# A written-out order of work for a two-layer image network on one Trainium2 core is replaced by another

## The chip, the cores and the metric

The kernel runs on one core of one Trainium2 chip. The metric is the device time of one execution, in microseconds (us). The core has five engines with an instruction queue each: TensorE (PE in the rows), ScalarE (ACT), VectorE (DVE), GpSimd (POOL) and SyncE (SP, which only issues DMAs here). Each engine works through its own queue in order, and semaphores hold it where it needs another engine's result.

## What is computed

The input is 32 images of 96 channels by 56 x 56 positions, fp32. Two layers follow each other. Cut to what matters:

```
x = x + conv0(ln_c(x))      # expand 96->576, SiLU, 3x3 depthwise, SiLU, squeeze-excite, project to 96, + identity
t = t + ffn0(ln_t(t))       # 96->384->96 with operands rounded to fp8 (5,2), sums to fp16
x = x + conv1(ln_c(x))      # 1x1, group norm, GELU, 4 shifted 1x1 + GELU summed, group norm, 1x1
t = t + ffn1(ln_t(t))
```

Each normalisation needs one over a square root per position (or per group). It is computed on VectorE by a seed from the bit pattern and three Newton steps.

## The kernel before, in words

Images pass through the engines as through a pipeline. An image is cut into 8 tiles of 7 rows (392 positions); the work of one image is cut into steps such as `center_a 3` or `expand 0 5`. `load_x` brings an image in; `center_a`, `var_a`, `rstd_a`, `fetch_a` and `norm_a` are the first normalisation; `expand k t` is the 1x1 expansion of 128-channel chunk k; `dw k h j` is tap j of the depthwise convolution of half an image on VectorE (lines 856 and 859), `silu2 k h` its activation on ScalarE (742); `texp` and `tconv` do the rest of the channels' convolution on TensorE; `se1` to `se3` are the squeeze-excite gate; `proj` and `x1` end the first convolution. `up`, `quant`, `down`, `add` are the two feed-forward parts (index 0 and 1). `conv1`, `stats`, `gn 0`, `gelu1`, `shift`, `combo`, `fold`, `sum`, `gn 1`, `gn_weights`, `conv3`, `x2` are the second convolution. `center`, `var`, `rstd`, `fetch`, `norm` with a first index 0, 1, 2 are the other three normalisations.

A normalisation goes round through memory. TensorE sums the squares (`var`, line 511). VectorE makes the root in 12 small operations (`rstd`: line 827, 394, 397, then three times 382, 385, 387). SyncE writes it out with four DMAs (line 409), waits for them, and reads it back tile by tile, spread over 96 partitions (line 416). VectorE then multiplies (`norm`).

The shifted copies for `combo` are made by DMA: `shift t` is five issues on SyncE (lines 471, 475 and 479 for two of the three channel groups) into one of two buffers. `combo t` (line 663) is 12 matmuls into three PSUM banks; ScalarE takes each out with a GELU (line 810), `fold t` (673) adds them up in one of three ring banks, and ScalarE copies that out (814). `combo t+1` may write a bank only when the GELU of tile t has read it, and `shift t+2` may start only when `combo t` is done.

On GpSimd there are two kinds of steps: `norm_a`, which adds a tile of x and a normalised tile (line 1001, called the sums here) once VectorE's `norm_a` of the tile is done, and the clearing of the borders of `g`, three memsets (995 to 997). `save_s` on SyncE (496) writes each sum out.

What sets the order is a table of numbers, `TIMES`. For each engine it gives each step a planned time; one period of 10,000 units is one image. `timetable` sorts the steps of all 32 images by that number, `LEAD` tells which image a step belongs to in a period, and `with_banks` deals out the three ring banks of PSUM by the planned times of their readers. Nothing but the sequence that comes out of the sort is used: no engine waits for a planned time, only for semaphores. A ScalarE function of another table set makes the compiler put an `ACT_TABLE_LOAD` ahead of it; SiLU and GELU stand in different sets.

```
                plan[engine] += [(PERIOD * m + time, m - lead_of(family), step) for m in range(NIMG)]
        plan[engine].sort()
...
            bank = min(free, key=lambda b: free[b])
```

Of the kernel before, what the change touches and what calls it, by code (L numbers as in the profile page):

```python
# [48 lines left out]
        "save_s": (6456, 7078, 7232, 7410, 7684, 7737, 7794, 8398), "texp 0": (11803, 11912, 12045, 12071),
        "texp 1": (12393, 12616, 12761, 12864), "texp 2": (13722, 13815, 13896, 13976),  # L50
        "fetch_s": (17257, 17333, 19025, 19039, 19566, 19591, 20287, 20676), "rstd 0": (21298,),
        "fetch 0": (21449, 21469, 21745, 21801, 22028, 22091, 22241, 22366), "rstd 1": (22875,),
# [1149 lines left out]
```

How the kernel before makes its waits and increments, by code:

```python
    def wait_sums(pe, prev):  # L334
        if prev is None:
            return
        (name, *a), i = prev
        if name == "var_a":
            pe.wait_ge(sem["seed_a"], at(3 * (i + 1) + 1))
        elif a[0] == 0:
            pe.wait_ge(sem["seed_c"], at(3 * i + 1))
        else:
            pe.wait_ge(sem["seed_b"], at(3 * (2 * (i - 1) + a[0] - 1) + 1))
# [1 line left out]
    def wait_bank(pe, prev):  # L346
        if prev is None:
            return
        (name, *a), i = prev
        if name == "center_a":
            pe.wait_ge(sem["squared_a"], at(NT * (i + 1) + a[0] + 1))
        elif name == "center":
            L, t = a
            pe.wait_ge(sem["squared_b" if L else "squared_c"], at(NT * (2 * (i - 1) + L - 1 if L else i) + t + 1))
        elif name == "expand":
            k, t = a
            pe.wait_ge(sem["activated1"], at(N_EXP * (i + (k < AHEAD)) + NT * k + t + 1))
        elif name == "texp":
            pe.wait_ge(sem["t_activated"], at(N_TE * i + SLOTS * a[0] + a[1] + 1))
        elif name == "tconv":
            pe.wait_ge(sem["t_activated2"], at(N_TC * i + PH * a[0] + a[1] + 1))
        elif name == "down":
            pe.wait_ge(sem["down_evacuated"], at(NT * (2 * (i - 1 - a[0]) + a[0]) + a[1] + 1))
        elif name == "fold":
            pe.wait_ge(sem["z_stored"], at(NT * (i - 1) + a[0] + 1))
        elif name == "se1":
            pe.wait_ge(sem["se_scalar"], at(2 * i + 1))
        elif name == "se2":
```

## Time and profile before

| | |
|---|---|
| median of 3 runs | 7031.78 us (7015.9 to 7036.94) |
| the profiled execution's own time | 7010.7 us |
| its span | 7008.9 us |
| TensorE busy (matmul) | 5784.1 us, 83% |
| VectorE busy | 5549.2 us, 79% |
| ScalarE busy | 4280.4 us, 61% |
| GpSimd busy | 337.2 us, 5% |
| mean granted TensorE clock | 0.943 of full speed |

Busy time counts instructions on the engine. "Idle before" is time in which an engine had nothing running, with what ended it. SPq rows are issues of DMAs on SyncE; an issue occupies the queue for the time shown, and the data land later.

### The profile page before, as it was taken

The page shows a single profiled execution, that of the slowest core. Times are in us where ns is not written, and L with a number is a line of the kernel's source. Part 1 is how long each engine was busy: PE and PEld are TensorE (multiplying, and loading weights), DVE is VectorE, ACT ScalarE, POOL GpSimd, SP SyncE. Part 2 cuts the span into 40 slices and gives each one's busy share as a digit, 9 for nine tenths or more (in the row PEclk, how much of TensorE's full clock was granted, in tenths as well). Part 3 has the DMA queues.
Part 4 walks back from the last instruction along what each step waited for, and adds up shares of the span by engine and source line. Part 5 has one row for each costly group of instructions (what it writes and reads, how often), then busy time and mean ns, then how long its engine had stood idle before and what let it go on. Part 6 is the DMA issues. An engine that isn't in the chain of part 4 may idle for free. (4 is left out here: it accounts for less than half of the span.)

```text
span 7008.9 us, 111308 instructions
## 1 busy us (share of the span) xinstructions
PE 5784.1 (83%) x40192; PEld 2345.7 (33%) x40192; DVE 5549.2 (79%) x9325; ACT 4280.4 (61%) x7549; POOL 337.2 (5%) x366
## 2 busy tenths in 40 slices
PE   2788888888898888888888888888888888888875
PEld 0233333333333333333333333333333333333332
DVE  5778887788887778887888888788888878887763
ACT  1456766666766656766666766656766656766654
POOL 1000000000000000000000000000000000000000
PEclk9899999999999999999999999999999999999997
DMA  1223323333323333323333323233323333323322
GB/s 40 60 73 86 87 75 85 79 78 88 89 73 87 78 80 87 88 74 86 79 80 87 89 74 88 76 80 87 89 75 86 81 76 87 89 72 87 79 59 63
DMA packets 395480, 556.44 MB, mean 79 GB/s; under 512 B 71490, under 2 KB 391427, under 8 KB 391771
## 3 DMA queue, kind: packets, MB, share of 16 engines
q1 hardware_dynamic: 394940, 549.32, 31.0%
q8 instruction: 330, 5.41, 0.3%
q14 instruction: 210, 1.72, 0.1%
HBM read 233.66 MB, written 78.68 MB: 45 GB/s over the span
## 5 line engine op out<-in xcount | busy, mean ns | idle before, releaser
L859 DVE SCALAR_TENSOR_TENSOR conv<-mid,w_dw,conv 128x1568 f32<-128x1568 f32 x1536 | 2837.6, 1847 | 28.1
L663 PE MATMUL b_banks<-shifted,w_combo 128*32 128x392 f32 x6144 | 637.4, 539 | 280.6 <-DMA shifted<-g 233.5
L535 PE MATMUL bank<-xc_a,w_exp 128*128 128x392 f32 x1536 | 706.3, 570 | 187.1 <-DVE xc_a L842 120.3
L583 PE MATMUL bank<-conv,w_proj_gated 128*96 128x392 f32 x2048 | 729.8, 499 | 5.9 <-DVE w_proj_gated L871 5.9
L598 PE MATMUL bank<-x,centering 128*96 128x392 f32 x1536 | 655.8, 519 | 92.0 <-ACT phases L722 52.7
L775 ACT ACTIVATE hidden<-b_banks 128x1176 f16<-128x1176 f32 x512 | 590.5, 1153 | 179.0 <-PE b_banks L618 175.8
L782 ACT ACTIVATE hidden<-hidden 128x1176 fp8e5<-128x1176 f16 x512 | 604.5, 1188 | 44.9 <-PE bank L627 24.5
L715 ACT ACTIVATE mid<-bank 128x392 f32<-128x392 f32 x768 | 381.1, 497 | 373.8 <-PE bank L535 350.5
L691 ACT ACTIVATE g<-bank 96x392 f32<-96x392 f32 x512 | 254.0, 496 | 520.9 <-PE bank L598 467.8
L742 ACT ACTIVATE conv<-conv,bn_affine 128x1568 f32<-128x1568 f32 x192 | 324.9, 1692 | 329.1 <-DVE conv L859 328.7
L914 DVE TENSOR_SCALAR hidden<-hidden,b_q 128x392 f16<-128x392 f16 x1536 | 395.0, 313 | 131.1 <-ACT hidden L775 130.8
L535 PEld LDWEIGHTS bank<-xc_a,w_exp 128*128 128x128 f32 x1536 | 286.9, 210 | 508.3 <-issue 292.1
L557 PE MATMUL bank<-phases_on,w_toeplitz 128*32 128x392 f32 x4608 | 443.6, 531 | 4.0 <-DMA phases_on<-phases 4.0
L663 PEld LDWEIGHTS b_banks<-shifted,w_combo 128*32 128x32 f32 x6144 | 212.4, 116 | 650.7 <-DMA shifted<-g 410.2
L1001 POOL TENSOR_TENSOR x<-x,xc_a 96x392 f32<-96x392 f32 x256 | 317.7, 1246 | 2291.6 <-DVE xc_a L842 2291.6
L583 PEld LDWEIGHTS bank<-conv,w_proj_gated 128*96 128x96 f32 x2048 | 321.3, 163 | 298.2 <-issue 257.2
L557 PE MATMUL bank<-phases,w_toeplitz 128*32 128x392 f32 x4608 | 411.6, 494 | 1.6 <-ACT phases L722 1.0
L627 PE MATMUL bank<-hidden,w_q 128*96 128x392 fp8e5 x1536 | 353.4, 340 | 63.6 <-ACT hidden L782 45.9
L618 PE MATMUL b_banks<-xn,w_q 128*128 128x392 fp8e5 x1536 | 346.0, 334 | 65.6 <-ACT hidden L775 37.8
L842 DVE TENSOR_TENSOR xc_a<-xc_a,r_a 96x392 f32<-96x392 f32 x256 | 167.6, 665 | 261.0 <-DMA r_a<-rstd_row_a 260.7
L733 ACT ACTIVATE conv<-bank,bn_affine 128x392 f32<-128x392 f32 x384 | 261.0, 680 | 178.8 <-PE bank L557 178.4
L544 PE MATMUL bank<-xc_a,w_exp 128*32 128x448 f32 x3072 | 348.5, 548 | 22.1 <-ACT phases L722 16.7
(157 smaller groups left out, 7926.6 us busy)
## 6 DMA issues: line engine op xcount, KB each, us to landing
phases_on<-phases SPq DMA_DIRECT2D x768, 101.5 KB, 2.6
...
shifted<-g SPq DMA_DIRECT2D x256, 199.5 KB, 2.9
...
r_a<-rstd_row_a SPq DMA_DIRECT2D x256, 147.0 KB, 2.9
x_plus_norm<-x SPq DMA_DIRECT2D x256, 147.0 KB, 2.6
r_a<-x_plus_norm SPq DMA_DIRECT2D x256, 147.0 KB, 2.3
```

Source lines behind the costliest of these rows:

```text
L535: mm(ring[bank][:, 0:TW], WEXP[:, 128 * k:128 * k + 128], xc_tile(t, 128), start=True, stop=True)\
L544: last = mm(ring[bank][32 * q:32 * q + 32, 0:EROWS * WW], WEXP[:, m0:m0 + 32], xc_phase(q, h), start=True, stop=True)
L557: last = mm(ring[bank][32 * p:32 * p + 32, 0:TW], TWZ[:, (3 * g + dx) * 2 + r % 2, :], phase_rows(EB if r < 2 else FB, p, QH, dx), start=( ...
L583: mm(o, WPS[:, k, :], tile(conv(k, t // NTH, parity), t % NTH, 128), start=(k == 0), stop=False)
L598: mm(ring[bank][0:C, 0:TW], CEN[:, :], tile(XFULL[1 - parity if L else parity], t, 128), start=True, stop=True)\
L627: last = mm(ring[bank][0:C, 0:TW], W2Q[:, f, c, :], Q8[t % 2][:, c, :], start=(c == 0), stop=(c == NHC - 1))
L663: last = mm(rows(PB[32 * u:32 * u + 32, m, 0:TW]), WC[:, u // 2, 32 * m:32 * m + 32], SH[t % 2][:, u, :].rearrange("p (h w) -> p h w", w=G ...
L715: f(mid_rows((k + (k < AHEAD) + parity) % 2, 1 + ROWS * t, ROWS), rows(ring[bank][:, 0:TW]), ACT.Silu)\
L775: f(Y16[t % 2][:, :, :], PB[:, 0:NHC, 0:TW], ACT.Copy).then_inc(sem["up_evacuated"], 1)
L782: f(Q8[t % 2][:, :, :], Y16[t % 2][:, :, :], ACT.Copy, saturate=False)\
L859: v.scalar_tensor_tensor(out=acc, in0=src, scalar=WDW[:, k, j:j + 1], in1=acc, op0=ALU.mult, op1=ALU.add).then_inc(sem["convolved"], 1)
L914: last = v.tensor_scalar(Y16[t % 2][:, c, :], Y16[t % 2][:, c, :], B1Q[:, g, c:c + 1], 0.0, ALU.add, ALU.max)
```

## The change

Only the table `TIMES` is replaced, on all five engines (lines 48 to 122). No instruction of the program is written otherwise: `ITERS` is 3 on both sides, so every root still has its nine Newton operations behind the first three. The number of instructions of a kind is the same on TensorE, VectorE, GpSimd and SyncE. The sequence on GpSimd is the same too. Two of the rows, and the shortest table whole:

```
     "SP": {
-        "load_x": (2489,), "rstd_a": (6044,), "fetch_a": (6093, 6329, 6392, 6436, 6587, 6728, 6856, 7150),
+        "load_x": (1832,), "rstd_a": (4902,), "fetch_a": (4931, 5374, 5857, 5900, 6400, 6627, 6900, 6929),
...
-        "shift": (24280, 24537, 24766, 24807, 24939, 25277, 25313, 25954), "rstd 2": (28475,),
+        "shift": (24665, 24876, 24982, 25058, 25721, 25722, 26264, 26463), "rstd 2": (28520,),
...
     "POOL": {
-        "norm_a": (4007, 4903, 5096, 5325, 5773, 6384, 8893, 9938), "gn 0": (23979,)},
+        "norm_a": (12718, 12775, 12862, 12887, 12912, 13053, 16342, 17167), "gn 0": (27816,)},
```

**SyncE, around the write of `rstd_row_a`** (the root of `rstd_a`; `shifted` are the copies for `combo`, `r_a` the root read back, `x_plus_norm` the stored sums). Before:

```order
L471 DMA shifted<-g 32x4x399
L475 DMA shifted<-g 32x399
L479 DMA shifted<-g 32x3x399
L475 DMA shifted<-g 32x399
L479 DMA shifted<-g 32x3x399
L409 DMA rstd_row_a<-rstd_a 8x98 x4
L416 DMA r_a<-rstd_row_a 96x392 x4
L496 DMA x_plus_norm<-x 96x392
L416 DMA r_a<-rstd_row_a 96x392 x3
```

and with the new table, from the last issue of `shift 1` on:

```order
L479 DMA shifted<-g 32x3x399
L409 DMA rstd_row_a<-rstd_a 8x98 x4
L416 DMA r_a<-rstd_row_a 96x392
L471 DMA shifted<-g 32x4x399
L475 DMA shifted<-g 32x399
L479 DMA shifted<-g 32x3x399
L475 DMA shifted<-g 32x399
L479 DMA shifted<-g 32x3x399
```

Before, all eight shifts stand ahead of the write of the root; now two do, and six stand behind it, with reads of `r_a` among them.

**VectorE, from the root of `rstd_a` to the first products with it** (`conv` are taps of the depthwise convolution, `xc_a` the product of `norm_a`, `bn_stats` the step `sum`). Before:

```order
L387 SCALAR_TENSOR_TENSOR rstd_a<-newton_a,rstd_a 128x98
L859 SCALAR_TENSOR_TENSOR conv<-mid,w_dw,conv 128x1568 x4
L979 BN_STATS bn_stats<-g 96x6
L859 SCALAR_TENSOR_TENSOR conv<-mid,w_dw,conv 128x1568
L842 TENSOR_TENSOR xc_a<-xc_a,r_a 96x392
L859 SCALAR_TENSOR_TENSOR conv<-mid,w_dw,conv 128x1568
L979 BN_STATS bn_stats<-g 96x6
L842 TENSOR_TENSOR xc_a<-xc_a,r_a 96x392
L979 BN_STATS bn_stats<-g 96x6
L842 TENSOR_TENSOR xc_a<-xc_a,r_a 96x392
```

and now:

```order
L387 SCALAR_TENSOR_TENSOR rstd_a<-newton_a,rstd_a 128x98
L859 SCALAR_TENSOR_TENSOR conv<-mid,w_dw,conv 128x1568 x3
L842 TENSOR_TENSOR xc_a<-xc_a,r_a 96x392
L859 SCALAR_TENSOR_TENSOR conv<-mid,w_dw,conv 128x1568
L856 TENSOR_SCALAR conv<-mid,w_dw 128x1568
L859 SCALAR_TENSOR_TENSOR conv<-mid,w_dw,conv 128x1568 x4
L842 TENSOR_TENSOR xc_a<-xc_a,r_a 96x392
L859 SCALAR_TENSOR_TENSOR conv<-mid,w_dw,conv 128x1568 x2
L842 TENSOR_TENSOR xc_a<-xc_a,r_a 96x392
```

The root itself now stands 3 taps behind `gn 0`, not 12, and taps, not `sum`, stand between the products.

**ScalarE, the second half of the combos** (`gelus` and `hidden` are written by the GELUs of `combo` 4, 6 and 5, 7; `g` by `fold`, `mid` by `expand`, `conv` by `silu2`). Before:

```order
L810 ACTIVATE hidden<-b_banks 128x392 x3
L742 ACT_TABLE_LOAD
L742 ACTIVATE conv,pool_sums<-conv,bn_affine 128x1568
L814 ACTIVATE g<-bank 96x392
L810 ACT_TABLE_LOAD
L810 ACTIVATE gelus<-b_banks 128x392 x3
L814 ACTIVATE g<-bank 96x392
L810 ACTIVATE hidden<-b_banks 128x392 x3
L715 ACT_TABLE_LOAD
L715 ACTIVATE mid<-bank 128x7x56
```

and now:

```order
L742 ACTIVATE conv,pool_sums<-conv,bn_affine 128x1568
L810 ACT_TABLE_LOAD
L810 ACTIVATE gelus<-b_banks 128x392 x3
L814 ACTIVATE g<-bank 96x392
L715 ACT_TABLE_LOAD
L715 ACTIVATE mid<-bank 128x7x56
L747 ACTIVATE x<-bank,x 24x1
L810 ACT_TABLE_LOAD
L810 ACTIVATE hidden<-b_banks 128x392 x3
L715 ACT_TABLE_LOAD
L715 ACTIVATE mid<-bank 128x7x56
```

Before, one image has 6 table loads; now it has 10, all ten between `gn 0` and `gn 1` (189 in the whole program before, 311 now). On TensorE, five more steps of `expand 0`, `se2` and a `texp` now stand ahead of `gn 1`, and `proj 0` right behind it.

## Rows read from the trace of the kernel before

**Rows 1.** The page: busy time of each engine, share of the span, instructions
```profile
PE 5784.1 (83%) x40192; PEld 2345.7 (33%) x40192; DVE 5549.2 (79%) x9325; ACT 4280.4 (61%) x7549; POOL 337.2 (5%) x366
```
**Rows 2.** VectorE's first step of the gate (`se2`, line 863), once per image
```profile
L863 DVE TENSOR_TENSOR gate<-bank,b_se x32: 148/150/156, 257.3 to 6775.3; 128x5 f32<-128x5 f32 x32
```
**Rows 3.** Windows: start:end and length, PE, PEld, DVE, ACT, POOL busy, PEclk, DMA share, GB/s
```profile
3000.00:3210.00 210.00, 180.06 (x1256) 73.39 (x1254) 170.89 (x290) 133.26 (x235) 10.14 (x11) 0.94 0.32 82
3137.00:3193.00 56.00, 39.38 (x374) 15.26 (x373) 44.63 (x62) 37.82 (x65) 6.59 (x5) 0.84 0.49 110
```
**Rows 4.** Waits: engine and line <- who was waited for: total us, times, longest
```profile
DVE xc_a L842 <- DMA r_a<-rstd_row_a: 260.7, 73, 10.2
PE b_banks L663 <- DMA shifted<-g: 233.5, 151, 9.2
PE sums_b L646 <- DVE gn_small L946: 171.7, 64, 6.6
PE bank L535 <- DVE xc_a L842: 120.3, 60, 20.0
```
**Rows 5.** Timeline of VectorE: start, us, instruction, [idle before <- releaser]
```profile
3141.08 0.15 DVE L966 TENSOR_TENSOR gn_small<-v_l,gn_small 96x1 f32<-96x1 f32 x1
...
3165.07 0.26 DVE L387 SCALAR_TENSOR_TENSOR rstd_a<-newton_a,rstd_a 128x98 f32<-128x98 f32 x1
...
3182.37 0.56 DVE L842 TENSOR_TENSOR xc_a<-xc_a,r_a 96x392 f32<-96x392 f32 x1 [7.39 <-DMA r_a<-rstd_row_a]
...
3185.09 0.89 DVE L842 TENSOR_TENSOR xc_a<-xc_a,r_a 96x392 f32<-96x392 f32 x1
...
3192.31 0.37 DVE L946 BATCH_NORM_AGGREGATE gn_small<-bn_stats 96x2 f32<-96x48 f32 x1
```
**Rows 6.** Timeline of SyncE's queue, issues of DMAs
```profile
3144.16 0.64 SPq L471 DMA_DIRECT2D shifted<-g  x1
...
3176.12 1.56 SPq L409 DMA_DIRECT2D rstd_row_a<-rstd_a  x4
3178.80 0.78 SPq L416 DMA_DIRECT2D r_a<-rstd_row_a  x2
```
**Rows 7.** Timeline of TensorE, 3182 to 3202
```profile
3182.99 0.93 PE L535 MATMUL bank<-xc_a,w_exp 128*128 128x392 f32 x2 [1.42 <-DVE xc_a L842]
3186.04 1.67 PE L535 MATMUL bank<-xc_a,w_exp 128*128 128x392 f32 x2 [2.13 <-DVE xc_a L842]
...
3192.73 0.48 PE L646 MATMUL sums_b<-gn_small,mean_w 96*96 96x1 f32 x2 [2.77 <-DVE gn_small L946]
...
3201.87 1.27 PE L573 MATMUL bank<-x 24*128 24x1 f32 x10
```
**Rows 8.** Timeline of ScalarE around a table load
```profile
3150.18 0.19 ACT L733 ACTIVATION_READ_ACCUMULATOR conv<-bank,bn_affine 128x1 f32 x1
3150.40 1.28 ACT L810 ACT_TABLE_LOAD   x1
3151.69 1.28 ACT L810 ACTIVATE gelus<-b_banks 128x392 f32<-128x392 f32 x3
```
**Rows 9.** Groups of instructions: busy us, mean ns | idle before <- releasers
```profile
L715 ACT ACTIVATE mid<-bank 128x392 f32<-128x392 f32 x768 | 381.1, 497 | 373.8 <-PE bank L535 350.5 <-DVE conv L859 17.8
L742 ACT ACTIVATE conv<-conv,bn_affine 128x1568 f32<-128x1568 f32 x192 | 324.9, 1692 | 329.1 <-DVE conv L859 328.7
L804 ACT ACTIVATE g<-g,gn_small 96x784 f32<-96x784 f32 x128 | 126.0, 1032 | 6.4 <-DVE gn_small L966 6.0
```
**Rows 10.** Timeline of GpSimd, the first two sums of an image
```profile
3183.01 2.55 POOL L1001 TENSOR_TENSOR x<-x,xc_a 96x392 f32<-96x392 f32 x1 [52.48 <-DVE xc_a L842]
3186.07 1.01 POOL L1001 TENSOR_TENSOR x<-x,xc_a 96x392 f32<-96x392 f32 x1 [0.50 <-DVE xc_a L842]
```
**Rows 11.** Lines 859 and 842 on VectorE: duration ns minimum/median/maximum
```profile
L859 DVE SCALAR_TENSOR_TENSOR conv<-mid,w_dw,conv x1536: 1825/1850/2481, 134.0 to 6748.8; 128x1568 f32<-128x1568 f32 x192
L842 DVE TENSOR_TENSOR xc_a<-xc_a,r_a x256: 539/561/1370, 124.3 to 6572.6; 96x392 f32<-96x392 f32 x128
```

More of the change, by code:

```diff
@@ L47 @@
     "SP": {
-        "load_x": (2489,), "rstd_a": (6044,), "fetch_a": (6093, 6329, 6392, 6436, 6587, 6728, 6856, 7150),
[L49 to L52, printed above, removed]
@@ L53 @@
-        "fetch 1": (23421, 23468, 23500, 23694, 23795, 23804, 23816, 24004),
-        "shift": (24280, 24537, 24766, 24807, 24939, 25277, 25313, 25954), "rstd 2": (28475,),
-        "fetch 2": (29254, 29708, 30046, 30181, 30549, 30641, 30643, 30686),
-        "store": (31436, 31483, 31621, 31905, 32012, 32030, 32068, 32260)},
-    "PE": {
-        "center_a": (4070, 4733, 4772, 5057, 5214, 5262, 5266, 5383),
-        "var_a": (4752, 5199, 5201, 5275, 5309, 5403, 5603, 5866),
[6 rows of a table removed]
-        "proj": (18219, 18289, 18966, 19097, 19214, 19315, 19579, 20019),
[7 rows of a table removed]
-        "combo": (25552, 25585, 25836, 26019, 26230, 26289, 26408, 26488),
[6 rows of a table removed]
@@ L81 @@
-    "ACT": {
-        "center_a": (4379, 4389, 4571, 4828, 4851, 5099, 5146, 5402),
[13 rows of a table removed]
-        "combo": (25304, 25315, 25637, 25816, 26032, 26199, 26239, 26348),
-        "fold": (25540, 26080, 26131, 26183, 26218, 26295, 26694, 26722),
[4 rows of a table removed]
-    "DVE": {
-        "rstd_a": (6141,), "norm_a": (6569, 6723, 6864, 7166, 7202, 7462, 7998, 8010),
[17 rows of a table removed]
+        "load_x": (1832,), "rstd_a": (4902,), "fetch_a": (4931, 5374, 5857, 5900, 6400, 6627, 6900, 6929),
+        "save_s": (5677, 6677, 6723, 6855, 7082, 7091, 7815, 8098), "texp 0": (8799, 9304, 10303, 10366),
@@ new lines @@
+        "texp 1": (11310, 11671, 11721, 12321), "texp 2": (13348, 13418, 13488, 13551),
+        "fetch_s": (17458, 17933, 18453, 18458, 18703, 18742, 19029, 19049), "rstd 0": (20616,),
+        "fetch 0": (20784, 20831, 20837, 20843, 21157, 21301, 21302, 21694), "rstd 1": (22328,),
+        "fetch 1": (23260, 23290, 23343, 23381, 23422, 23460, 23664, 24595),
+        "shift": (24665, 24876, 24982, 25058, 25721, 25722, 26264, 26463), "rstd 2": (28520,),
+        "fetch 2": (28558, 28645, 28683, 28721, 29544, 30077, 30293, 30355),
@@ new lines @@
+        "store": (30260, 30746, 30809, 30936, 31085, 31161, 31687, 31821)},
+    "PE": {
+        "center_a": (2930, 3375, 3666, 3845, 3961, 3995, 3996, 4332),
+        "var_a": (3849, 3859, 3904, 4073, 4097, 4335, 4336, 4364),
[14 rows of a table added]
+        "combo": (24379, 24390, 24475, 24764, 25147, 25452, 25664, 26125),
[6 rows of a table added]
+    "ACT": {
+        "center_a": (3485, 3805, 3930, 4351, 4378, 4548, 4596, 4650),
[13 rows of a table added]
+        "combo": (25176, 25335, 25376, 25414, 25883, 26039, 26540, 26805),
+        "fold": (25278, 25839, 25946, 26117, 26395, 26634, 27208, 27210),
[4 rows of a table added]
@@ L121 @@
+    "DVE": {
+        "rstd_a": (4562,), "norm_a": (4688, 5183, 5364, 5669, 5951, 6083, 6315, 6746),
[17 rows of a table added]
     "POOL": {
-        "norm_a": (4007, 4903, 5096, 5325, 5773, 6384, 8893, 9938), "gn 0": (23979,)},
+        "norm_a": (12718, 12775, 12862, 12887, 12912, 13053, 16342, 17167), "gn 0": (27816,)},
 }
```

107 rows, old and new, of the table TIMES are left out of this document.

## Prediction

> **What bounds the kernel now.** I read the busy times first, then windows of one image, then the waits, then the timeline of the stretch where the waits are. No engine is full: TensorE is busy 83%, VectorE 79%, ScalarE 61% [rows 1]. The gate's first step runs once per image, from 257.3 to 6775.3 us, so an image takes (6775.3 - 257.3) / 31 = 210.3 us [rows 2]; filling and emptying the pipeline are the other 491 us. In 210 us TensorE works 180 and VectorE 171 [rows 3]. So the time is set by TensorE's 180 us plus the 30 in which it stands still, and a new order can only take from those 30; VectorE's 39 idle us cost something only where TensorE waits for it.
>
> TensorE's idle time is not spread evenly. In the 56 us around the stretch from `gn 0` to `gn 1` it works 39.4, and so stands still 16.6 us [rows 3], over half of all. The waits say why: for shifted copies 233.5 us in the run (7.3 an image), for the statistics of the two group norms 171.7 (5.4), for the first products `xc_a` 120.3 (3.8) [rows 4]. Behind the last stands SyncE. VectorE has the root of `rstd_a` at 3165.3 [rows 5], but SyncE is issuing shifts from 3144.16 on, forty DMAs of 0.64 us and less, and comes to the root only at 3176.12; the first product starts at 3182.37, after 7.39 us of waiting [rows 5, 6]. That is the place the new order rearranges most.
>
> **The change part by part.** Let T be the end of `gn 0` on VectorE, 3141.2. Before, `gn 1` begins at 3192.3 [rows 5], T + 51.1. I follow the new order through this stretch with the durations of the rows.
>
> 1. SyncE. Shifts 0 and 1 go out as before, till about T + 9.7. The root now stands 3 taps behind `gn 0`: 5.6 us, then 3.4 for its 12 operations, T + 9.4. SyncE writes it at once, waits as before (3176.12 to 3178.80, 2.7 us [rows 6]) and reads tile 0 at T + 12.4. The first product can run at T + 16, where it ran at T + 41.2 [rows 5]. The price: shift 2 starts at T + 12.8 where it started at T + 10.5, so the six later shifts are 2.3 us late, and the reads of `r_a` among them (0.3 to 0.4 each) add about 1.5.
>
> 2. VectorE. The 7.39 us wait goes, since 3 taps (5.6 us) now cover most of the way through memory. That is not on the path by itself; it lets `expand 0` start earlier. The two waits of `expand 0` for products, 1.42 + 2.13 [rows 7], go with it, and five more of these steps (0.92 us each, from 0.93 in [rows 7]), `se2` (1.27 [rows 7]) and one `texp` (0.9) fill TensorE's gaps before `gn 1`. Two pieces leave the stretch, a `tconv` (2.2) and a `var_a` (0.4). Net, 4.6 + 1.3 + 0.9 - 2.6 = 4.2 us of TensorE's work per image moves from where it is full to where it waits.
>
> 3. ScalarE. Here the change costs. Ten table loads stand in the stretch, not six; a load takes 1.28 us [rows 8], so 5.1 us more, and a further `silu2` comes in (1.69 + 0.19 [rows 8, 9]) for a `tconv` that leaves (0.9). ScalarE's work there: 24 GELUs, 8 copies of `fold`, 6 of `expand` and 6 operations of `center_a` at 0.50 at most 11.9 + 3.9 + 3.0 + 2.9, three `silu2` 5.6, four `gelu1` 4.1 [rows 9], small ones 0.5, loads 12.8; in all 44.7 us, where the same count gives 36.4 before (the window has 37.8 [rows 3]). Followed through, `combo 1` waits for ScalarE's extra `silu2` and load till T + 13.5; `combo 4` starts at T + 25.4; `silu2 2 1` and a load hold `se1` and `combo 7` till T + 39.8; the last `fold` is out at T + 51.3, and `gn 1` begins at T + 52.3: 1.2 us later than before.
>
> After a load the next function starts at once: the load ends at 3151.68 and the GELU begins at 3151.69, so a switch costs 1.3 us [rows 8]. The Trainium skill (ScalarE: Activation LUTs, What ACT_TABLE_LOAD costs) states 1.28 us for the load and a drain of about 1.38 behind it, 2.66 for each switch. The load agrees with this trace; the drain does not show in it.
>
> 4. The group norms. Before, `gn 1` cost TensorE 2.77 us at its first step [rows 7]; now `texp 0 0` and `expand 0 6` stand ahead and `proj 0` behind. For `gn 0` a tap no longer stands between the last `stats` and the sum. Of the 5.4 us an image [rows 4] I take 1.5 outside the stretch's length.
>
> 5. The sums on GpSimd. Beside a tap a sum took 2.55 us, beside short steps 1.01 [rows 10]; a product next to a sum took 0.89 where 0.56 is the median, a tap at most 2.48 where 1.85 is [rows 5, 11]. Eight sums now meet mostly taps: from 0 to 8 x 0.63 = 5.0 us an image on VectorE, against 0.8 before (mean 665 less 561 ns, times 8). I take no difference: VectorE waits in this stretch anyway, and nobody waits long for the sums. The Trainium skill (SBUF — State Buffer, SBUF: two separate sides) says that a VectorE operation with two SBUF inputs and a GpSimd operation that reads SBUF exclude each other for the whole instruction. A tap has two such inputs, so by that rule moving the sums from products to taps frees nothing, which speaks against this part; the 2.55 us agree.
>
> 6. The roots. No operation of a root is added or removed, so this is worth nothing. Were two Newton operations of each really gone, it would be 4 x 2 x 0.3 + 2 x 2 x 0.19 = 3.2 us of VectorE an image.
>
> 7. The rest of the image (159 us before). I compared the order there without finding a place that is clearly better or worse: the taps of the first half now lie among the products of `norm 2`, where VectorE waited, but outside the stretch TensorE works 180.1 - 39.4 = 140.7 of 154 us [rows 3], and a wait of VectorE's mostly costs nothing. I take 0, with 3 us to each side.
>
> The sum for an image: +1.2 (stretch longer) - 4.2 (work no longer to be done outside it) - 1.5 = -4.5 us. Times 31 that is -140; filling and emptying I leave as they are. From the profiled execution's 7010.7 us this gives 6871. The median of the runs, 7031.8, lies 21 above that execution, so I put the forecast between, at 6880: 1.9% below 7010.7.
>
> **The rivals.**
>
> A. Slower: ScalarE sets the stretch. It would have 44.7 us of work in 52, and the loop combo - GELU - next combo and the three ring banks leave it little room to work ahead. If the loads and the extra `silu2` all lie on the loop, the stretch grows by 5.1 + 1.9 = 7.0 us, and the fillers gain nothing, since ScalarE must empty their banks too: +7.0 - 1.5 = +5.5 an image, 7181; if the fillers still count, 7.0 - 4.2 - 1.5 = +1.3, 7051. It decides once ScalarE idles under about 4 us in the stretch. For it: the loads are certain. Against: before, ScalarE idled 18 of the 56 us. I take 7110 for this case.
>
> B. No change: SyncE is only reshuffled. What the early root gains (3.6 us of waiting for products) is lost again by the late shifts (2.3 + 1.5 = 3.8). Then 7010, give or take 20.
>
> C. Faster than forecast: the rest of the image also loses waits, half of TensorE's 13 us there (154 - 140.7). That is -4.5 - 6.5 = -11 an image, 6670.
>
> D. A switch costs more than the load itself, as where something must drain first. With 1.4 us more for each of four added loads, +5.5 on the path, the sum becomes +1.0 an image, 7042. The rows show 0.01 us behind the load, so this has 1 in 100. It is what the drain of the Trainium skill's page would do.
>
> **How the numbers follow.** About 0.3%, 21 us, is what a measurement can tell from no change. Forecast 0.50 (6780 to 6970), A 0.23, B 0.11, C 0.15, D 0.01. Faster: 0.50 + 0.15 + 0.02 of B = 0.67. Same: 0.09 of B + 0.01 of A = 0.10. Slower: 0.22 of A + 0.01 = 0.23. The range is 6690 to 7110: it leaves out the slower half of A (0.11) and the faster half of C (0.07). The forecast's own range is 6780 to 6970.
>
> **What would show it.** Right: an image takes about 206 us; VectorE's 7.39 us wait for `r_a` is near 1; the root is written within 2 us of its end; TensorE works 42 to 43 us in the stretch from `gn 0` to `gn 1`, which is 51 to 54 long; ScalarE has 311 table loads of 1.28 us, and idles some 7 us of the stretch. Wrong: a stretch of 57 us or more with waits of TensorE for GELUs (A), waits for shifted copies grown by as much as those for products fell (B), or a gain outside the stretch (C).

## The result, and the profile after

| | before | after |
|---|---|---|
| median of 4 runs on one chip | 7034.36 us | 6854.82 us (6850.41 to 6863.16) |
| ratio, 95% interval | | 0.9749 (0.9734 to 0.9764) |
| the profiled execution's span | 7008.9 us | 6852.4 us |
| mean granted TensorE clock | 0.943 | 0.959 |

The new order is 2.5% faster. The prediction said faster, 1.9%, at 6880 us. The two profiled executions are 2.2% apart, since that of before, at 7010.7 us, is faster than any of the four runs of its kernel (7015.9 to 7041.9). Up to the experiments the text compares these two. The page after, first part, which answers to [rows 1]:

```profile
PE 5730.9 (84%) x40192; PEld 2277.5 (33%) x40192; DVE 5543.4 (81%) x9325; ACT 4409.0 (64%) x7671; POOL 452.6 (7%) x366
```

ScalarE has 122 instructions more (the table loads) and 129 us more of busy time, GpSimd 115 us more for the same 366 instructions, and TensorE 53 us less for the same 40192 matmuls. Each of the three is taken up below.

Where in the run did the time go? The end of `gn 0` on VectorE (T of the prediction) comes once per image. Cut at the first and at the 31st of these, the run falls into filling, 30 whole images, and emptying (start:end and length; PE, PEld, DVE, ACT, POOL busy; PEclk, DMA share, GB/s). First before:

```profile
0.00:396.10 396.10, 211.54 (x1396) 81.09 (x1400) 259.38 (x326) 124.97 (x248) 32.58 (x33) 0.90 0.19 50
396.10:6718.20 6322.10, 5384.14 (x37666) 2189.90 (x37662) 5153.71 (x8671) 4010.42 (x7072) 304.30 (x330) 0.95 0.32 82
6718.20:7008.90 290.70, 188.39 (x1142) 74.71 (x1134) 136.09 (x330) 144.98 (x230) 0.30 (x3) 0.81 0.26 64
```

and after:

```profile
0.00:391.80 391.80, 209.49 (x1433) 81.30 (x1433) 260.37 (x328) 126.38 (x249) 33.15 (x33) 0.91 0.20 50
391.80:6563.40 6171.60, 5336.27 (x37630) 2124.45 (x37626) 5149.26 (x8671) 4135.18 (x7191) 419.16 (x330) 0.97 0.33 84
6563.40:6852.40 289.00, 185.11 (x1134) 71.79 (x1134) 133.72 (x328) 147.41 (x232) 0.30 (x3) 0.82 0.27 64
```

The 30 images are 150.5 us shorter: 5.0 an image, from 210.7 to 205.7. The filling is 4.3 shorter and the emptying 1.7. In the middle TensorE's work falls by 1.6 us an image and its idle time from 6322.1 - 5384.1 = 938.0 us to 835.3, 3.4 an image. So nearly a third of the gain, as TensorE's time is booked, is no waiting: the same matmuls take less time. (The gate's rows of [rows 2] are no fair mark for a comparison of the two orders. The last of them stood 57.1 us behind the last `gn 0` used here and stands 41.4 behind it now, so a cut there gives 5.4 us an image, and an emptying that seems 14 us longer.)

The next cut is by stage, two windows of one image on each side: from the end of `gn 0` to `gn 1`, and from there to the next `gn 0`. Before:

```profile
3141.20:3192.30 51.10, 35.66 (x350) 13.39 (x342) 41.46 (x44) 34.62 (x59) 6.55 (x5) 0.87 0.52 118
3192.30:3353.10 160.80, 145.08 (x910) 60.39 (x914) 130.27 (x247) 99.20 (x178) 3.59 (x7) 0.97 0.26 70
```

After:

```profile
2862.70:2913.10 50.40, 37.24 (x338) 13.83 (x334) 42.25 (x47) 41.00 (x66) 12.65 (x7) 0.90 0.58 141
2913.10:3067.60 154.50, 139.68 (x924) 56.61 (x922) 129.49 (x244) 96.68 (x175) 1.31 (x4) 1.00 0.25 66
```

The same two cuts over all 30 images, as the sums that close the two answers. The stretches, before and after:

```profile
sum 1520.40, PE 1038.52 PEld 384.27 DVE 1244.94 ACT 1034.11 POOL 196.61; mean PE 34.62 PEld 12.81 DVE 41.50 ACT 34.47 POOL 6.55
sum 1530.90, PE 1147.28 PEld 426.76 DVE 1265.75 ACT 1236.39 POOL 379.91; mean PE 38.24 PEld 14.23 DVE 42.19 ACT 41.21 POOL 12.66
```

and the rest of each image, before and after:

```profile
sum 4801.70, PE 4345.62 PEld 1805.63 DVE 3908.76 ACT 2976.31 POOL 107.69; mean PE 144.85 PEld 60.19 DVE 130.29 ACT 99.21 POOL 3.59
sum 4640.70, PE 4188.99 PEld 1697.69 DVE 3883.51 ACT 2898.79 POOL 39.25; mean PE 139.63 PEld 56.59 DVE 129.45 ACT 96.63 POOL 1.31
```

The stretch takes 50.7 us before and 51.0 after: it is not shorter. TensorE worked 34.6 of it and now 38.2, so it stands idle 12.8 us there where it stood 16.1, 3.3 less. The rest of the image went from 160.1 to 154.7, and this is the whole gain: TensorE has 5.2 us less work there (3.6 of it stands in the stretch now), and its idle time there is what it was (15.2 and 15.1). The granted clock of the rest rose from 0.97 to 0.99 of full speed. Less idle time in the stretch (3.3), less outside it (0.1) and less work in all (1.6) are the 5.0 us.

Where most of the work became cheaper is one line. TensorE's `expand` (line 535), as a group (busy us, mean ns | idle before <- releasers), before:

```profile
L535 PE MATMUL bank<-xc_a,w_exp 128*128 128x392 f32 x1536 | 706.3, 570 | 187.1 <-DVE xc_a L842 120.3 <-ACT mid L715 57.3 <-ACT phases L722 6.7
```

and after:

```profile
L535 PE MATMUL bank<-xc_a,w_exp 128*128 128x392 f32 x1536 | 654.9, 525 | 110.1 <-DVE xc_a L842 34.0 <-ACT mid L715 25.7 <-ACT sq_b L692 19.9
```

51.4 us less for the same 1536 matmuls, the largest fall of any line. That it nearly equals TensorE's 53.2 in the whole run is chance, since other lines changed both ways: the matmuls of a `combo` (line 663) went from 539 to 580 ns on average, half of those of line 557 (`tconv`) from 531 to 494. In the timeline of before, three steps of `expand 0` stand right behind `gn 1`, where TensorE has just waited and the granted clock is 0.50, the lower of its two levels (1.2 GHz); after, three such steps stand ahead of `gn 1` and run at the upper (2.4 GHz) at nearly twice the speed. Over 30 images of before, the `expand` matmuls in the first 6 us behind the start of `gn 1` took 862 ns on average; after, none stands there, and those in the stretch take 551. The rows of the three steps, before and after:

```profile
3194.30 4.27 PE L535 MATMUL bank<-xc_a,w_exp 128*128 128x392 f32 x6
```

```profile
2908.08 2.30 PE L535 MATMUL bank<-xc_a,w_exp 128*128 128x392 f32 x6 [0.35 <-DVE gate L863]
```

**The hand-made timeline of the stretch**, against the trace of after. With T = 2862.7, the end of `gn 0`, SyncE, then VectorE, ScalarE and TensorE read:

```profile
2864.38 0.65 SPq L471 DMA_DIRECT2D shifted<-g  x1
...
2871.74 1.44 SPq L409 DMA_DIRECT2D rstd_row_a<-rstd_a  x4
...
2874.31 0.31 SPq L416 DMA_DIRECT2D r_a<-rstd_row_a  x1
...
2875.01 0.59 SPq L471 DMA_DIRECT2D shifted<-g  x1
```

```profile
2871.29 0.26 DVE L387 SCALAR_TENSOR_TENSOR rstd_a<-newton_a,rstd_a 128x98 f32<-128x98 f32 x1
...
2877.11 0.56 DVE L842 TENSOR_TENSOR xc_a<-xc_a,r_a 96x392 f32<-96x392 f32 x1
...
2907.77 0.16 DVE L863 TENSOR_TENSOR gate<-bank,b_se 128x5 f32<-128x5 f32 x1 [1.80 <-PE bank L573]
...
2913.08 0.37 DVE L946 BATCH_NORM_AGGREGATE gn_small<-bn_stats 96x2 f32<-96x48 f32 x1
```

```profile
2872.51 1.28 ACT L810 ACT_TABLE_LOAD   x1
2873.80 0.89 ACT L810 ACTIVATE gelus<-b_banks 128x392 f32<-128x392 f32 x2
...
2898.10 1.70 ACT L742 ACTIVATE conv<-conv,bn_affine 128x1568 f32<-128x1568 f32 x1 [1.07 <-DVE conv L859]
...
2904.69 0.25 ACT L747 ACTIVATE x<-bank,x 24x1 f32<-24x1 f32 x1
```

```profile
2887.99 2.18 PE L663 MATMUL b_banks<-shifted,w_combo 128*32 128x392 f32 x24 [0.62 <-DMA shifted<-g]
...
2901.85 3.19 PE L663 MATMUL b_banks<-shifted,w_combo 128*32 128x392 f32 x24 [0.84 <-ACT gelus L810]
```

| milestone | by hand | measured |
|---|---|---|
| root written by SyncE | T + 9.4 to 9.7 | T + 9.0 |
| read of tile 0 | T + 12.4 | T + 11.6 |
| shift 2 | T + 12.8 | T + 12.3 |
| first product | T + 16 | T + 14.4, with no wait |
| combo 4 | T + 25.4 | T + 25.3 |
| combo 7 | T + 39.8 | T + 39.2 |
| `gn 1` | T + 52.3 | T + 50.4 |

The root is written 0.2 us after its end (2871.29 + 0.26), where it had waited 10.8 us behind forty issues [rows 5, 6]. The first product no longer waits. Of the waits of [rows 4], after:

```profile
DVE xc_a L842 <- DMA r_a<-rstd_row_a: 122.6, 97, 5.3
PE b_banks L663 <- DMA shifted<-g: 257.8, 151, 9.3
PE b_banks L618 <- ACT hidden L775: 116.8, 133, 2.3
```

VectorE waits 138 us less for `r_a`, while TensorE waits 24 us more for shifted copies, the price of the interleaving. The 171.7 us for `gn_small` of line 946 [rows 4] have shrunk to 8.5; a wait of `up` (line 618) for ScalarE's `hidden`, 37.8 us before, has grown to 116.8.

### The profile page after: what moved, and what is told of

Read it like the earlier page. It is cut to its first block, busy times and chain, and to the rows that moved or that the text cites. A ratio compares the mean times of both kernels' runs of the same rounds, so it can differ in the third digit from the quotient of the medians.

```text
span 6852.4 us, 111430 instructions
## 1 busy us (share of the span) xinstructions
PE 5730.9 (84%) x40192; PEld 2277.5 (33%) x40192; DVE 5543.4 (81%) x9325; ACT 4409.0 (64%) x7671; POOL 452.6 (7%) x366
## 4 chain that ended last, share of the span: by engine, by line
PE 45%; DVE 31%; ACT 10%; DMA 6%; issue 5%; SPq 4%; DVEq 0%; ACTq 0%; POOL 0%; POOLq 0%
DVE conv L859 16%; PE bank L583 10%; PE bank L598 6%; PE bank L557 4%; PE bank L535 3%; PE bank L585 3%; PE b_banks L682 3%; PE b_banks L639 2%; PE bank L544 2%; DVE hidden L914 2%; PE b_banks L663 2%; ACT hidden L782 2%; PE b_banks L618 2%; DVE xn L906 2%; DVE x L924 2%
## 5 line engine op out<-in xcount | busy, mean ns | idle before, releaser
L859 DVE SCALAR_TENSOR_TENSOR conv<-mid,w_dw,conv 128x1568 f32<-128x1568 f32 x1536 | 2893.7, 1884 | 20.4
L663 PE MATMUL b_banks<-shifted,w_combo 128*32 128x392 f32 x6144 | 681.1, 580 | 311.9 <-DMA shifted<-g 257.8
L535 PE MATMUL bank<-xc_a,w_exp 128*128 128x392 f32 x1536 | 654.9, 525 | 110.1 <-DVE xc_a L842 34.0
L782 ACT ACTIVATE hidden<-hidden 128x1176 fp8e5<-128x1176 f16 x512 | 607.4, 1186 | 39.4 <-DVE hidden L914 39.2
L1001 POOL TENSOR_TENSOR x<-x,xc_a 96x392 f32<-96x392 f32 x256 | 433.2, 1693 | 1729.9 <-DVE xc_a L842 1729.9
L722 ACT ACTIVATE phases<-bank 128x448 f32<-128x448 f32 x384 | 208.5, 543 | 515.5 <-PE bank L544 422.6
L618 PE MATMUL b_banks<-xn,w_q 128*128 128x392 fp8e5 x1536 | 348.4, 336 | 133.8 <-ACT hidden L775 116.8
L544 PE MATMUL bank<-xc_a,w_exp 128*32 128x448 f32 x3072 | 381.7, 555 | 58.2 <-ACT phases L722 47.6
L557 PE MATMUL bank<-phases_on,w_toeplitz 128*32 128x392 f32 x4608 | 411.5, 494 | 0.2 <-ACT conv L733 0.2
L691 ACT ACTIVATE xc<-bank 96x392 f32<-96x392 f32 x256 | 125.5, 490 | 434.5 <-PE bank L598 301.9
L535 PEld LDWEIGHTS bank<-xc_a,w_exp 128*128 128x128 f32 x1536 | 259.0, 193 | 377.6 <-issue 245.1
```

Source lines behind the costliest of these rows:

```text
L535: mm(ring[bank][:, 0:TW], WEXP[:, 128 * k:128 * k + 128], xc_tile(t, 128), start=True, stop=True)\
L544: last = mm(ring[bank][32 * q:32 * q + 32, 0:EROWS * WW], WEXP[:, m0:m0 + 32], xc_phase(q, h), start=True, stop=True)
L557: last = mm(ring[bank][32 * p:32 * p + 32, 0:TW], TWZ[:, (3 * g + dx) * 2 + r % 2, :], phase_rows(EB if r < 2 else FB, p, QH, dx), start=( ...
L618: last = mm(PB[:, c, 0:TW], W1Q[:, f, 128 * c:128 * c + 128], XN8[t % 2][:, :], start=True, stop=True)
L663: last = mm(rows(PB[32 * u:32 * u + 32, m, 0:TW]), WC[:, u // 2, 32 * m:32 * m + 32], SH[t % 2][:, u, :].rearrange("p (h w) -> p h w", w=G ...
L782: f(Q8[t % 2][:, :, :], Y16[t % 2][:, :, :], ACT.Copy, saturate=False)\
```

## The experiments

Twelve kernels. Each changes single numbers of the table, or one line, of the kernel after or before, so that a step stands elsewhere in one or two queues. The columns are the median, the ratio to before on the same chip with its interval, the period (from the first to the 31st end of `gn 0`, over 30), and in it TensorE's work and idle time per image, from the same window. The runs come from several chips, on which the kernel before had medians of 7017 to 7034 us. So kernels are compared by the ratio; the last three columns, each from one execution, can differ by some 0.5 us for that alone.

| run | us | ratio | period | work | idle |
|---|---|---|---|---|---|
| before | 7034 | 1 | 210.7 | 179.5 | 31.3 |
| after | 6855 | 0.9749 (0.9734 to 0.9764) | 205.7 | 177.9 | 27.8 |
| e2_root_early (of before) | 6983 | 0.9936 (0.9913 to 0.9959) | 209.7 | 180.1 | 29.5 |
| e3_gn0_first (of before) | 7103 | 1.0109 (1.0087 to 1.0131) | 213.9 | 178.8 | 35.1 |
| e1_root_late | 7140 | 1.0163 (1.0142 to 1.0184) | 215.0 | 180.1 | 34.9 |
| k_read_behind_shift2 | 6955 | 0.9898 (0.9882 to 0.9915) | 208.9 | 178.6 | 30.3 |
| i_fillers_behind_gn1 | 7010 | 0.9987 (0.9977 to 0.9998) | 210.8 | 180.4 | 30.4 |
| j_tconv_inside | 6848 | 0.9759 (0.9736 to 0.9782) | 205.5 | 176.5 | 29.0 |
| f4_four_loads | 7036 | 1.0020 (1.0008 to 1.0032) | 211.6 | 180.6 | 30.9 |
| f3_combo7_late_se1 | 6949 | 0.9908 (0.9891 to 0.9926) | 208.8 | 180.3 | 28.6 |
| f12_six_loads | 6931 | 0.9882 (0.9861 to 0.9902) | 208.0 | 178.4 | 29.5 |
| f2_late_silu2 | 6867 | 0.9781 (0.9758 to 0.9804) | 206.0 | 177.9 | 28.0 |
| g_small_sums | 6834 | 0.9747 (0.9724 to 0.9770) | 205.0 | 177.3 | 27.6 |
| h_two_newton | 6830 | 0.9726 (0.9704 to 0.9749) | 204.8 | 177.7 | 27.2 |

### One part of the change alone: SyncE's root (e2)

In the kernel before, the write of the root and its first read are moved ahead of the last two shifts.

```diff
-        "load_x": (2489,), "rstd_a": (6044,), "fetch_a": (6093, 6329, ...
+        "load_x": (2489,), "rstd_a": (5300,), "fetch_a": (5301, 6329, ...
```

> The order before, with one thing moved on SyncE alone: the write of the root of rstd_a and the read of its first tile stand ahead of shifts 6 and 7, not behind them. My theory (term 1 and 2 of the sum): VectorE's wait of 7.4 us for r_a and TensorE's two waits for products (1.4 + 2.1 us) go, and shifts 6 and 7 come 3 us later; I expect 0 to -2 us an image, 6950 to 7010 us against a before of about 7010. Rival B (SyncE is only reshuffled: late shifts cost what the early root gains): 7010 within 20 us.

The first product comes at T + 34.3 instead of T + 41.2, and its waits drop from 260.7 to 160.1 us; the rows of the first two products:

```profile
2949.69 0.56 DVE L842 TENSOR_TENSOR xc_a<-xc_a,r_a 96x392 f32<-96x392 f32 x1
2956.00 0.56 DVE L842 TENSOR_TENSOR xc_a<-xc_a,r_a 96x392 f32<-96x392 f32 x1 [3.51 <-DMA r_a<-rstd_row_a]
```

The period falls by 1.1 us, as expected, and the stretch from 50.7 to 49.5 on average. So this part of the move of SyncE's root is neither a mere reshuffling (rival B) nor, alone in the old order, the bulk of the gain: a fifth of it by the period, a quarter by the ratio.

### One part alone: `gn 0` ahead of the last tap (e3)

```diff
-        ... "gn 0": (25175,),
+        ... "gn 0": (25010,),
```

> The order before, with gn 0 on VectorE moved ahead of the last tap of dw 1 1, as the new table has it: one tap, 1.85 us, no longer stands in front of the first group norm. If that wait of TensorE is on the path (term 4), the time falls by 1.5 to 1.9 us an image: 6955 to 6965 us against 7010. If it is off the path, no change.

It became slower by 1.1%, 3.2 us an image; the expectation was wrong. ScalarE's `silu2 1 1` stands ahead of `gelu1` in the old order and waits for the tap that was now put behind `gn 0`. This wait holds up ScalarE, and with it the GELUs whose group norm had just been hurried:

```profile
3176.17 1.70 ACT L742 ACTIVATE conv<-conv,bn_affine 128x1568 f32<-128x1568 f32 x1 [6.34 <-DVE conv L859]
```

The new table puts `silu2 1 1` behind `gelu1`. That costs table loads, and it takes this step out of the way when `gn 0` goes first on VectorE. That the two edits belong together is read from this wait; no run makes both in the old order.

### The root late, and the read late (e1, k)

Both of the kernel after. e1 moves SyncE's write and first read of the root behind shift 3; k leaves the write and moves only the first read behind shift 2.

```diff
-        "load_x": (1832,), "rstd_a": (4902,), "fetch_a": (4931, 5374, ...
+        "load_x": (1832,), "rstd_a": (5060,), "fetch_a": (5061, 5374, ...
```

```diff
-        "load_x": (1832,), "rstd_a": (4902,), "fetch_a": (4931, 5374, ...
+        "load_x": (1832,), "rstd_a": (4902,), "fetch_a": (4983, 5374, ...
```

> The new order, with the write of the root of rstd_a and the read of its first tile on SyncE moved back behind shift 3 (behind shift 1 before): two shifts, 6.4 us, stand ahead of it again. My theory: the first product comes 6 us later, the taps behind it and silu2 too, and the time rises by 2 to 5 us an image, 6915 to 7010 against about 6855. Rival (the early root is worth nothing, shifts 2 and 3 come 2.7 us earlier): 6855 or a little less.

> The new order, with one number changed: on SyncE the read of the first tile of r_a stands behind shift 2, not ahead of it. SyncE then issues shift 2 while the root is being written, 1.8 us earlier, and reads tile 0 some 2 us later. If the shifts are what holds the stretch (TensorE waits 8.0 us for them there), up to 1.8 us an image less: 6800 to 6840, ratio 0.967 to 0.973. If the root's way to the products is the longer one, as the late root (4.2% slower) suggests, 1 to 3 us an image more: ratio 0.980 to 0.989. This run is also the try at a version that beats both.

The first product, first of e1 and then of k:

```profile
2997.52 0.56 DVE L842 TENSOR_TENSOR xc_a<-xc_a,r_a 96x392 f32<-96x392 f32 x1 [9.87 <-DMA r_a<-rstd_row_a]
```

```profile
2918.11 0.56 DVE L842 TENSOR_TENSOR xc_a<-xc_a,r_a 96x392 f32<-96x392 f32 x1 [4.84 <-DMA r_a<-rstd_row_a]
```

In e1 it comes at T + 24.3, on average 9.6 us later than after (24.3 against 14.8), the stretch is 60.5 us long, and the period grows by 9.3: more than expected, and 2.2 of them are more time for TensorE's same work, at a granted clock of 0.83 in the stretch instead of 0.89. In k the product of this image comes at T + 19.25, but on average at T + 18.3, 3.5 later. The delay reaches `se2` unchanged (first step of the gate at T + 48.6 instead of T + 45.2 on average); the stretch grows to 54.3 us, the period by 3.2. By the ratio, 0.9898, k lies just beyond the slower of its two expectations. The expected earlier shift did not come: shift 2's first issue is at T + 12.95 with the read behind it and T + 12.3 with the read ahead. Its buffer comes free only when `combo 0` is done, and SyncE's waits for that (line 467) rose from 37.5 to 65.1 us in the run.

So this chain sets the stretch: root, SyncE's write and read, first product, ten more taps and `silu2`, the gate, `gn 1`. The trace of after has no wait on record at the first product in the image shown, and yet each microsecond of delay there is worth 0.9 to 1.0 of period. SyncE's place for the root is therefore a condition for the rest of the change, worth far more there than in the old order (1.1), where other things held the stretch.

### The fillers behind `gn 1` (i)

Of the kernel after: the four steps `expand 0` 3 to 6 and `texp 0 0` go behind `gn 1`, and the two last `fold` copies are moved so that they don't wait for them.

```diff
-        "expand 0": (4853, 5512, 6134, 6250, 6252, 6330, 6871, 7379), "texp 0": (6825, 7264, 9741, 9748),
+        "expand 0": (4853, 5512, 6134, 6900, 6901, 6902, 6903, 7379), "texp 0": (6904, 7264, 9741, 9748),
...
-        "fold": (25278, 25839, 25946, 26117, 26395, 26634, 27208, 27210),
+        "fold": (25278, 25839, 25946, 26117, 26395, 26634, 27085, 27086),
```

> The new order, with the fillers taken back out of the stretch between the group norms: expand 0 3 to 0 6 and texp 0 0 stand behind gn 1 on TensorE, not ahead of it, and fold 6 and 7 ahead of expand 0 3 on ScalarE. My theory (term 2): about 4.6 us of TensorE's work goes back outside, the folds come some 2 us earlier, so the time rises by 2 to 4 us an image, 6915 to 6980. Rival (the stretch's work is no matter, its length is): gn 1 comes 2 us earlier and the time falls, 6790 to 6855.

5.1 us an image are lost, more than expected, and the ratio is back at 0.9987. The windows of one image, as above:

```profile
2921.40:2971.10 49.70, 33.69 (x326) 12.33 (x318) 42.12 (x47) 39.60 (x63) 12.66 (x7) 0.90 0.58 143
...
2971.10:3132.20 161.10, 146.07 (x920) 59.71 (x921) 129.17 (x244) 97.52 (x177) 1.30 (x4) 0.97 0.24 63
```

The stretch is about as long as it was (49.7 us), and TensorE works 3.6 us less in it (33.7 against 37.2). The rest of this image is 161.1 us long instead of 154.5, with 6.4 us more work in it (146.1 against 139.7), at a granted clock of 0.97 instead of 1.00 in these two images: what is moved out of the stretch costs more where it lands. The group of `expand` shows the second half of the price, 59 us in the run that vanish in the kernel after:

```profile
L535 PE MATMUL bank<-xc_a,w_exp 128*128 128x392 f32 x1536 | 714.2, 574 | 82.3 <-DVE xc_a L842 32.1 <-ACT sq_b L692 19.9 <-ACT mid L715 13.1
```

Over 30 images the loss is 2.5 us of work (180.4 against 177.9) and 2.6 of idle time for each; the stretch is 1.1 us shorter (49.9) and the rest 6.2 longer (160.9). Without the fillers the gain is gone. But the losses of single moves don't add up to it: a late root (e1) costs 9.3.

### One more filler (j)

Of the kernel after: `tconv 2 3`, one of the two pieces of work that the change takes out of the stretch, goes back into it.

```diff
-        ... "tconv 2": (13285, 13293, 13549, 13565), "se1": (16104,),
+        ... "tconv 2": (13285, 13293, 13549, 14370), "se1": (16104,),
...
-        ... "tconv 2": (13317, 13414, 13522, 13740), "silu2 1": (13568, 15111),
+        ... "tconv 2": (13317, 13414, 13522, 15112), "silu2 1": (13568, 15111),
```

> The new order, with one more filler: tconv 2 3 stands behind var_a 7 on TensorE, where it waits 3.7 us for the first shift, and behind silu2 1 1 on ScalarE (no table load more). 2 us of TensorE's work move from ahead of gn 0 into a wait. By my theory -1.5 to -2 us an image, if ScalarE's 0.9 us ahead of the first GELUs don't count: 6790 to 6820, ratio 0.966 to 0.970. Rival: ScalarE comes 0.9 us later to combo 0 and the stretch is longer by as much: 0.972 to 0.977.

No change: 0.9759 against 0.9749, the intervals overlap. The expected gain of 1.5 to 2 us did not come, and the ratio lies in the rival's range, though the stretch grew by 0.4 us only (51.4), not 0.9. TensorE's work falls by 1.4 us an image, all of it in the combos (580 to 547 ns a matmul, at a granted clock of 0.94 in the stretch instead of 0.89), and its idle time grows by 1.2. The rest of the image lost 2.2 us of TensorE's work (139.6 to 137.4) but only 0.6 of its length: there TensorE now waits 16.7 us instead of 15.1. So neither less work nor a fuller stretch shortens the period by itself: a filler pays only if the place it leaves gets shorter.

### Fewer table loads (f4, f3, f12, f2)

All of the kernel after. Two steps of `silu2` and `combo 7` on ScalarE are moved so that SiLU and GELU alternate less: all three moves (f4, 127 loads instead of 311), `combo 7` alone (f3, 251 loads), the two of `silu2` (f12, 187 loads), the second of these alone (f2).

```diff
-        ... "silu2 1": (13568, 15111),
+        ... "silu2 1": (13568, 14515),
-        "silu2 2": (15691, 16435), "se1": (16781,), "se3": (17081,),
+        "silu2 2": (16379, 16435), "se1": (16781,), "se3": (17081,),
...
-        "combo": (25176, 25335, 25376, 25414, 25883, 26039, 26540, 26805),
+        "combo": (25176, 25335, 25376, 25414, 25883, 26039, 26540, 26779),
```

> The new order, with four table loads an image instead of ten: silu2 1 1 ahead of the first gelu1, silu2 2 0 behind expand 0 0, the GELUs of combo 7 ahead of expand 0 1 and se1. 7.7 us less work an image on ScalarE in the stretch between the group norms. If ScalarE's loads are on the path there (term 3 and rival A), 1.2 to 5 us an image come back: 6700 to 6815 against 6855. If TensorE and the DMAs of the shifts set the stretch, no change within 20 us; the later se1 could cost up to 1 us an image, 6885.

> The new order, with one step moved on ScalarE: the GELUs of combo 7 ahead of expand 0 1 and se1, which saves two of the ten table loads (2.6 us) and makes se1 about 4 us later. The three moves together cost 181 us (7036 against 6855), and in that trace se1 ran 4.6 us later. If the gate's chain (se1, se2, se3, then the expands and sums behind it) is what sets the end of the stretch, this move alone brings most of it: 6960 to 7040. If the late silu2 2 0 or the banks did it, this one is near 6855.

> The new order, with silu2 1 1 ahead of the first gelu1 and silu2 2 0 behind expand 0 0: six table loads an image instead of ten, 5.1 us less on ScalarE, se1 left where it was. If the loads are hidden in ScalarE's waits for the combos (as in the trace of the new kernel, where the second combo waits for shifts anyway), within 25 us of 6855. If the loads are on the path (rival A), 1 to 4 us an image less, 6730 to 6820.

> The new order, with silu2 2 0 moved behind expand 0 0 on ScalarE, so that combo 4 no longer waits behind it and two of ten table loads go. The two moves that left six loads cost 1.35% together. If the first (silu2 1 1 ahead of gelu1, 1.9 us earlier on the way to the first shift) did all of it, this one is near or below 6855 (ratio 0.970 to 0.976); if the loads' places matter, it is 0.978 or more.

None is faster, though each saves 1.28 us a load. f4, with six loads fewer an image, loses all of the gain: its stretches are 56.9 us on average, `se1` comes at T + 47.7 instead of T + 42.6, and ScalarE idles 22.6 us of one, where it idles 9.8 in the kernel after. In f3 the stretch is 54.3, in f12 53.4. The expectations for f4 and f12, no change or faster, were both wrong; f3, expected to bring most of f4's loss if the gate's chain did it, brought 3.1 of 5.8 us. In f12, `gelu1` starts 2.25 us behind T and not 0.59, since a `silu2` and a load stand ahead of it:

```profile
2889.70 1.28 ACT L804 ACT_TABLE_LOAD   x1
2891.00 1.04 ACT L804 ACTIVATE g<-g,gn_small 96x784 f32<-96x784 f32 x1
```

f2 costs 0.3 us an image, which the intervals don't separate from nothing (0.9781, between its two expectations); of the 2.3 us that f12 costs, some 2.0 are then the place of `silu2 1 1` by subtraction. In f2 ScalarE has 2.6 us less work in a stretch and idles 2.9 more (12.7): these two loads stood in its waits. In the other three a step moves together with its loads, so they show that the place of the step costs more than the loads can be worth, and not what the loads cost by themselves. A step of 1.7 us in front of the wrong neighbour stood on the chain.

### Sums that hardly read SBUF (g)

Of the kernel after: GpSimd's sum works on 8 of the 392 columns, so that the rest of the stored sums is left out. It shows what the meeting of VectorE and GpSimd costs.

```diff
-                g.tensor_tensor(tile(XA, t), tile(XA, t), xc_tile(t), ALU.add)...
+                g.tensor_tensor(tile(XA, t)[:, 0:8], tile(XA, t)[:, 0:8], xc_tile(t)[:, 0:8], ALU.add)...
```

> The new order, with GpSimd's sums cut to 8 of the 392 columns of a tile (the x that is stored and read back lacks the other columns' normalised part): the cost of sums beside taps taken away. The trace of the new kernel has a tap at 1884 ns on average against 1847 before, 1.8 us an image. If that lies on the path, -1 to -2 us an image, 6795 to 6825; if VectorE has room for it, as I took in term 5, within 20 us of 6855.

The taps, products and sums, as groups, of the kernel after (to be read beside [rows 11], which gives minimum, median and maximum of before):

```profile
L859 DVE SCALAR_TENSOR_TENSOR conv<-mid,w_dw,conv 128x1568 f32<-128x1568 f32 x1536 | 2893.7, 1884 | 20.4
L1001 POOL TENSOR_TENSOR x<-x,xc_a 96x392 f32<-96x392 f32 x256 | 433.2, 1693 | 1729.9 <-DVE xc_a L842 1729.9
L842 DVE TENSOR_TENSOR xc_a<-xc_a,r_a 96x392 f32<-96x392 f32 x256 | 158.3, 619 | 122.8 <-DMA r_a<-rstd_row_a 122.6
```

and of g:

```profile
L859 DVE SCALAR_TENSOR_TENSOR conv<-mid,w_dw,conv 128x1568 f32<-128x1568 f32 x1536 | 2833.8, 1845 | 20.4
L1001 POOL TENSOR_TENSOR x<-x,xc_a 96x8 f32<-96x8 f32 x256 | 224.9, 878 | 1890.9 <-DVE xc_a L842 1890.8
L842 DVE TENSOR_TENSOR xc_a<-xc_a,r_a 96x392 f32<-96x392 f32 x256 | 142.9, 559 | 192.2 <-DMA r_a<-rstd_row_a 191.4
```

With the short sums a tap takes 1845 ns and a product 559. In the kernel after the sums cost VectorE (1884 - 1845) x 1536 = 60 us on taps and (619 - 559) x 256 = 15 on products; before, with means of 1847 and 665, 3 and 27. So with the sums moved among the taps, what they cost VectorE went from 30 to 75 us (an estimate, which takes the means of g as free of them). The ratio of g is that of after (0.9747, 0.9749): of the 75 us, 69 are taken back as waiting for `r_a`, 122.6 to 191.4.

### A root with two Newton steps (h)

Of the kernel after: one of the three Newton steps of every root is left out, so that a root has nine operations and not twelve.

```diff
-SEEDS, ITERS = 3, 3
+SEEDS, ITERS = 3, 2
```

> The new order, with two Newton steps in each root instead of three (nine operations with the seed instead of twelve; roots less exact by that step): 3 of 12 operations of 0.30 us in each of four roots and 3 of 0.19 us in each of two group norms, 4.7 us of VectorE an image. If all roots lie on the path: -4.7 an image, 6710. The group norms and rstd_a lie in or at the stretch (2.0 us of it): I expect -1.5 to -4 us an image, 6730 to 6810, ratio 0.958 to 0.969.

VectorE's busy time falls by 4.0 us an image, and the period by 0.9 in the trace, 0.5 by the ratio. That is less than expected, and the interval (0.9704 to 0.9749) overlaps that of after. So three quarters or more of a shorter root are hidden. Two operations fewer in each root, which the prediction prices at 3.2 us of VectorE (term 6), would be worth at most about 0.6 us an image by the same share (two of three operations; an estimate), below what a measurement can tell.

## Why the prediction was right, point by point

**What bounds the kernel.** Right: TensorE's work and its idle time in the stretch. 3.3 of the 3.4 us of idle time that went, went there.

**SyncE (1) and VectorE (2).** The hand-made timeline held within 0.8 us at the root, the read and shift 2, within 1.6 at the first product and within 0.7 at the combos. (Its T + 9.4 for the root is a small slip: its terms, 5.6 and 3.4, give 9.0, and the root ended at T + 8.9.) The stretch came out 1.9 shorter than put down for it in this image, and +0.4 against +1.2 on the average before. The step that moves work into the gaps, -4.2, measured 3.6 us more work in the stretch, and with +0.4 of length 3.3 less idle time; the prediction's own pair is -4.2 + 1.2 = -3.0. Experiment i, which takes the fillers out, confirms the mechanism. One number of this step was mis-set: TensorE "works 42 to 43 us in the stretch". The 39.4 from which it starts is of a window of 56 us [rows 3] that reaches beyond both group norms; the stretch itself had 34.6 on average, and has 38.2 now.

**ScalarE (3).** Right that 311 loads of 1.28 us come and that the next function starts at once (2872.51 + 1.28 = 2873.79; the GELU at 2873.80). ScalarE's work in the stretch was set at 44.7 us; it is 41.2 on average, so it idles 9.8 us and not 7. The stretch hardly grew (+0.4) though ten loads stand in it; f2 shows of two of them that they stand where ScalarE would wait.

**The group norms (4).** Wrong, in that the term is not there. The wait of 171.7 us [rows 4] is all but gone, but other waits took its place (line 618, and a wait of `var`, line 511, for ScalarE's `sq_a`, 8.7 us before and 66.6 now), and outside the stretch TensorE's idle time fell by 0.1 us an image, not 1.5.

**The term that was missing.** TensorE's work was held constant. It fell by 1.6 us an image, because some matmuls that ran at the lower clock level, behind a wait, now run at the upper. With it the measured sum is -3.3 - 0.1 - 1.6 = -5.0, against the forecast's -3.0 - 1.5 = -4.5. So the sum came near by luck in one respect: 1.4 us of the group norms that did not come were made good by 1.6 us of a term that was not in it. The mechanism that was forecast, work moved into the stretch's gaps, is the 3.3. The rows for the missing term were there: the clock of 0.84 in [rows 3] against 0.94 for the whole image.

**Filling and emptying.** Taken as unchanged, and nearly right: they are 4.3 and 1.7 us shorter. The prediction takes 31 images between the gate's rows; between ends of `gn 0` there are 30, so 150.5 + 6.0 = 156.5 us stand against its 140.

**The sums (5), the roots (6), the rest (7).** All three at nothing; g and h bear out the first two within what the intervals can tell. The third has no run of its own: outside the stretch TensorE's idle time stayed as it was. The bound of 0 to 5.0 us an image for the sums was well placed, VectorE pays 75 us in the run, 2.3 an image, and none of it shows in the time. The rule of the Trainium skill (SBUF — State Buffer, SBUF: two separate sides) that speaks against this part is that a VectorE operation with two SBUF inputs and a GpSimd operation that reads SBUF keep each other out. The durations agree with it (a sum at 1.69 us on average among taps, 1.25 before), and by g it decides nothing here.

**The rivals.** A, that ScalarE's loads set the stretch, is refuted: the stretch grew by 0.4 us and not 7, ScalarE idles 9.8 us in it, and the four kernels with fewer loads are equal or slower. B, that SyncE is only reshuffled, is refuted by e2, e1 and k. C, waits lost outside the stretch, did not come (0.1 of 6.5). D, a drain behind each load, is refuted by the row of 2872.51: the next function starts 0.01 us behind the load, which is the median of all 311 loads too.

No run is faster than the kernel after by more than the intervals allow: j computes the same and equals it, and g and h, which leave work out, gain 0.0 and 0.2%.
